# A three-layer graph network on one core: when VectorE reads a visit's sums, five buffers of one-hots, and GpSimd's scaling

## What is computed

```python
def _mean_agg(x, src, dst, n):
    msg_sum = jax.ops.segment_sum(x[src], dst, num_segments=n)
    cnt = jax.ops.segment_sum(jnp.ones((src.shape[0], 1), x.dtype), dst, num_segments=n)
    return msg_sum / jnp.maximum(cnt, 1.0)

def _sage_conv(x, src, dst, Wl, bl, Wr):
    agg = _mean_agg(x, src, dst, x.shape[0])
    return agg @ Wl.T + bl + x @ Wr.T
...
h = jnp.maximum(_layernorm(x, axis=-1), 0.0)
h = _sage_conv(h, src, dst, Wl0, bl0, Wr0)          # 128 -> 256
h = jax.nn.relu(_batch_norm(h, gamma0, beta0))
h = _sage_conv(h, src, dst, Wl1, bl1, Wr1)          # 256 -> 256
h = jax.nn.relu(_batch_norm(h, gamma1, beta1))
h = _sage_conv(h, src, dst, Wl2, bl2, Wr2)          # 256 -> 128
return x + jax.nn.log_softmax(h, axis=-1)
```

## Time and profile before

| | us |
|---|---|
| median of 3 runs (1485.67 to 1491.87) | 1490.81 |
| the profiled execution's own time | 1489.97 |
| its span, first to last instruction | 1488.2 |

### The profile page before, as it was taken

One profiled execution on the slowest core, in us unless ns is written; L12 is line 12 of the kernel. 1 busy time (PEld: TensorE's weight loads), 2 busy tenths in 40 slices (PEclk: granted clock), 3 DMA queues, 4 the chain that ended last, 5 costly groups with the idle time before them and its releaser, 6 DMA issues.

```text
span 1488.2 us, 36176 instructions
## 1 busy us (share of the span) xinstructions
PE 1330.0 (89%) x16035; PEld 855.4 (57%) x16035; DVE 603.8 (41%) x1131; ACT 519.4 (35%) x848; POOL 561.1 (38%) x562
## 2 busy tenths in 40 slices
PE   1387888898788889999999999999999899999997
PEld 1276777677677678665444444444446764444445
DVE  6977767677777984222011111111111211212223
ACT  4886766867687685441000000000000330000001
POOL 3313130321304000001766666665663015666650
PEclk9999989989999999999999999999999999999999
DMA  5234533543544354136667666665663479898983
GB/s 162 94 144 153 188 150 138 200 156 134 192 178 181 118 187 179 50 126 226 222 197 241 205 226 229 221 217 200 217 215 109 115 260 323 309 328 298 334 314 96
DMA packets 92007, 291.45 MB, mean 196 GB/s; under 512 B 17538, under 2 KB 53012, under 8 KB 88612
## 3 DMA queue, kind: packets, MB, share of 16 engines
q1 hardware_dynamic: 63596, 228.73, 42.9%
q0 software_dynamic: 21824, 55.44, 12.0%
q10 hardware_dynamic: 6424, 4.88, 1.1%
HBM read 197.78 MB, written 91.22 MB: 194 GB/s over the span
## 4 chain that ended last, share of the span: by engine, by line
PE 72%; issue 8%; ACT 7%; DMA 6%; DVE 4%; POOL 4%; ACTq 0%; SPq 0%; DVEq 0%; POOLq 0%
PE bank L1621 25%; PE bank L1198 14%; PE cells L1621 12%; PE cells L1188 5%; DMA hots<-table,src_i 3%; PE bank L1866 3%; ACT ring L652 3%; POOL hots L516 3%; PE cells L1233 2%; PE cells L1687 2%; PE bank L1624 2%; ACT junk L600 2%; DMA parts<-in_pairs_dram,last_i 1%; PE cells L1699 1%; PE bank L1206 1%
## 5 line engine op out<-in xcount | busy, mean ns | idle before, releaser
L516 POOL DMA_INDIRECT hots<-table,src_i x444 | 420.9, 948 | 458.1 <-DMA table<-parts 224.6
L1621 PE MATMUL bank<-ring,parts 128*128 128x500 f16 x2058 | 460.1, 373 | 0.0
L652 ACT CAST ring<-cells 128x980 f16<-128x980 f32 (+1 forms) x325 | 335.5, 1057 | 140.8 <-PE cells L1188 137.1
L1198 PE MATMUL bank<-ring,parts 64*128 64x250 f16 x4900 | 336.7, 279 | 14.3 <-issue 8.6
L1621 PEld LDWEIGHTS bank<-ring,parts 128*128 128x128 f16 x2058 | 191.9, 96 | 223.8 <-issue 9.4
L1198 PEld LDWEIGHTS bank<-ring,parts 64*128 64x128 f16 x4900 | 238.1, 98 | 39.2 <-issue 19.3
L877 DVE TENSOR_TENSOR hots<-iotas,tab 128x980 f16<-128x980 f16 (+3 forms) x262 | 247.4, 998 | 26.0 <-PE cells L1188 13.6
L1621 PE MATMUL cells<-ring,parts 128*128 128x500 f16 (+1 forms) x980 | 215.9, 373 | 0.0
L723 ACT ACTIVATE agmg<-cells,isp 128x124 f32<-128x124 f32 x20 | 7.3, 365 | 471.1 <-PE cells L1242 471.1
L1188 PE MATMUL cells<-hots 64*128 64x49 f16 x4670 | 110.0, 188 | 67.4 <-DVE hots L877 35.0
L1621 PEld LDWEIGHTS cells<-ring,parts 128*128 128x128 f16 (+1 forms) x980 | 90.9, 96 | 112.7 <-issue 9.0
(11 more groups left out here) (211 smaller groups left out, 1000.1 us busy)
## 6 DMA issues: line engine op xcount, KB each, us to landing
ring<-c_blocks SPq DMA_DIRECT2D x120, 750.0 KB, 6.1
c_blocks<-ring SPq DMA_DIRECT2D x25, 3062.5 KB, 10.7
ring<-c_blocks SPq DMA_DIRECT2D x40, 812.5 KB, 6.7
rcb<-rc_row SPq DMA_DIRECT2D x69, 125.0 KB
hots<-table,src_i POOLq DMA_INDIRECT x444
Z<-in_x_dram SPq DMA_DIRECT2D x4, 768.0 KB, 6.3
table<-parts SPq DMA_DIRECT2D x2, 1536.0 KB
table<-parts ACTq DMA_DIRECT2D x2, 1536.0 KB
```

The lines of the kernel that those rows point to most:

```text
L516: pool.indirect_dma_start(out=got[layer][:, 5 * (r % NGOT) + i, :], out_offset=None, in_=tables[layer], in_offset=bass.IndirectOffsetOnAxi ...
L652: act.copy(blk[c % 2][:, :, :].rearrange("p a (d g) -> p a d g", d=GD)[:, :, :, GPS * i:GPS * i + n], cells[t % 2][:, :, 0:n * NA].rearran ...
L1198: ins = pe.matmul(bank[2 + h][:, 0:BD], small[rows, a, part, :], blk[c % 2][rows, a, :], start=(a, part) == (0, 0), stop=(a, part) == (FUL ...
L1621: ins = pe.matmul(bank[b][:, 0:2 * BD].rearrange("p (s d) -> p s d", s=2), lhs, ring[0:r, :, BD * a:BD * a + BD], start=(a, part) == (0, 0 ...
```

## The change

- VectorE reads the sums of block c-2 in step 6 of visit c instead of step 2 (`dve_sums0`: copy and addition only). TensorE's wait in step 1 is as it was.
- The multiplication by the reciprocal counts goes to GpSimd (`mean0`, step 7 of visit c), with the semaphore `means` in place of `v_mean`; for the last block VectorE does it. The factor 1/1024 goes into the weights `wl[0]`, which VectorE scales beside `wr[0]`.
- NHOT is 5 instead of 4. Two of the buffers now lie in `early`, and two small arrays move (`grow` into `src_i`, `gspare` into `smp_i`).
- The table of a batch from the third on is made in steps 5, 6 and 7 of its visit, one instruction each, instead of all three in step 7.

Left out below are the hunks in which `v_mean` only becomes `means`, and the one that moves the two small arrays.

```diff
@@ -21,7 +21,7 @@
 EPS = 1e-5
 S0 = 1024.0
 GPH = 20
-NHOT = 4
+NHOT = 5
 NBT = 4
 NTAB = 8
 NG1 = 4
@@ -87,6 +87,8 @@
             chores.update({t0 + 18: ("rows", q + 1, 0), t0 + 31: ("windows", q + 1, 0), t0 + 33: ("ends", q + 1, 0), t0 + 41: ("tile", q + 1, 0),
                            t0 + 42: ("place", q + 1, 0), t0 + 46: ("table", q + 1, 0)})
 
+
+    table_at = {t + k: (k, chores[t][1]) for t in list(chores) if chores[t][0] == "table" for k in ((-2, -1, 0) if chores[t][1] > 1 else (0,))}
     turn_step = {c: t for t, (what, _, c) in chores.items() if what == "turn"}
 
     quarters = [(NA * k // 4, NA * (k + 1) // 4) for k in range(4)]
@@ -300,13 +302,14 @@
         xres = upper.rearrange("p (a f) -> p a f", a=NA)
         X = Z[:, 1, :].rearrange("p (a f) -> p a f", a=NA)
         HOT = GPH * (NA + P)
-        need = NBT * 256 + NBT * 3 * P + HOT // 2
-        early = upper if NA * 128 >= need + WE else sb("early", [P, need + WE])
+        need = NBT * 256 + NBT * 3 * P + HOT
+        early = upper if NA * 128 >= need else sb("early", [P, need])
         win = early[:, 0:NBT * 256].bitcast(I32).rearrange("p (w n two) -> p w n two", w=NBT, two=2)
         wrk = early[:, NBT * 256:NBT * (256 + 3 * P)].rearrange("p (k n e) -> p k n e", k=3, e=P)
-        hots = sb("hots", [P, NHOT - 1, HOT], F16)
-        hot = [early[:, NBT * (256 + 3 * P):need].bitcast(F16)] + [hots[:, k, :] for k in range(NHOT - 1)]
-        later = hots[:, :, :].rearrange("p k n -> p (k n)") if (NHOT - 1) * HOT >= 8960 else sb("later", [P, 8960], F16)[:, :]
+        hots = sb("hots", [P, NHOT - 2, HOT], F16)
+        hot = [early[:, need - HOT + HOT // 2 * k:need - HOT + HOT // 2 * (k + 1)].bitcast(F16) for k in range(2)] + \
+            [hots[:, k, :] for k in range(NHOT - 2)]
+        later = hots[:, :, :].rearrange("p k n -> p (k n)") if (NHOT - 2) * HOT >= 8960 else sb("later", [P, 8960], F16)[:, :]
         got = [None] + [later[:, 0:5 * NGOT * w].rearrange("p (s f) -> p s f", s=5 * NGOT) for w in rowf[1:]]
         agmg = sb("agmg", [P, 2, BD])
         gsum = sb("gsum", [P, 256])
@@ -532,7 +535,7 @@
             pool_ends(0)
             pool_rows(1)
             pool_windows(1)
-            for t in range(NST * NB):
+            for t in range(NST * (NB + 1)):
                 what, q, _ = chores.get(t, ("", 0, 0))
                 if what == "rows":
                     pool_rows(q)
@@ -542,6 +545,9 @@
                     pool_ends(q)
                 elif what == "place" and q > 1:
                     pool_place(q)
+                c, i = divmod(t, NST)
+                if c >= 2 and i == 7:
+                    mean0(pool, c - 2)
                 if t in ln_at and ln_at[t] in act_groups:
                     pool_lo(ln_at[t])
                 if t == TG - 20:
@@ -782,21 +788,27 @@
                 dve.tensor_scalar(wrk[:, 1, 0:n, HE * h:HE * h + HE], wrk[:, 0, 0:n, HE * h:HE * h + HE], float(h), -1024.0,
                                   ALU.is_equal, ALU.mult).then_inc(v_place, 1)
 
-        def dve_table(q, own):
+        def dve_table(q, k, own):
+
             n = batches[q][1] - batches[q][0]
             pen, hi = wrk[:, 1, 0:n, :], wrk[:, 2, 0:n, :].bitcast(I32)
+            c0, c1 = batches[q]
             if q > 1:
                 dve.wait_ge(p_place, 2 * (q - 1))
             else:
                 dve.wait_ge(v_place, 2 * (q + 1))
-            dve.wait_ge(v_tile, q + 1)
-            c0, c1 = batches[q]
-            dve.tensor_reduce(cntg[:, c0:c1, :], pen.rearrange("p n (d e) -> p n d e", d=GD), AX.X, ALU.add).then_inc(v_own, 1)
-            dve.wait_ge(v_own, own.up())
-            dve.scalar_tensor_tensor(pen, hi, 1024.0, pen, ALU.add, ALU.add).then_inc(v_own, 1)
-            own.up()
-            dve.scalar_tensor_tensor(wrk[:, 2, 0:n, :], hi, -128.0, win[:, 0:n, :, 0],
-                                     ALU.mult, ALU.add).then_inc(v_table, 1)
+            if k == -2 or q <= 1:
+                dve.tensor_reduce(cntg[:, c0:c1, :], pen.rearrange("p n (d e) -> p n d e", d=GD), AX.X, ALU.add).then_inc(v_own, 1)
+                own.up()
+            if k == -1 or q <= 1:
+                dve.wait_ge(v_tile, q + 1)
+                dve.wait_ge(v_own, own.n)
+                dve.scalar_tensor_tensor(pen, hi, 1024.0, pen, ALU.add, ALU.add).then_inc(v_own, 1)
+                own.up()
+            if k == 0:
+                dve.wait_ge(v_own, own.n)
+                dve.scalar_tensor_tensor(wrk[:, 2, 0:n, :], hi, -128.0, win[:, 0:n, :, 0],
+                                         ALU.mult, ALU.add).then_inc(v_table, 1)
 
         def loose_part(q):
 
@@ -878,7 +890,7 @@
                                         place.unsqueeze(2).to_broadcast((P, q, w, 2)), ALU.is_equal)
             ins.then_inc(v_hot, 1)
 
-        def dve_mean0(c, own):
+        def dve_sums0(c, own):
 
             mean = agm[:, c % 2, 0, :].rearrange("p (g d) -> p g d", d=GD)
             first, last = (bank[2 + h][:, 0:BD].rearrange("p (d g) -> p g d", d=GD) for h in range(2))
@@ -886,10 +898,12 @@
             dve.tensor_copy(mean, first).then_inc(v_own, 1)
             dve.wait_ge(v_own, own.up())
             dve.tensor_tensor(mean, last, mean, ALU.add).then_inc(v_halves, 1)
-            dve.wait_ge(v_halves, c + 1)
-            dve.wait_ge(d_rcb[c % 2], 16 * (c // 2 + 1))
-            dve.scalar_tensor_tensor(mean, mean, 1.0 / S0, rcb[:, c % 2, :].rearrange("p (g d) -> p g d", d=GD), ALU.mult,
-                                     ALU.mult).then_inc(v_mean, 1)
+
+        def mean0(eng, c):
+
+            eng.wait_ge(v_halves, c + 1)
+            eng.wait_ge(d_rcb[c % 2], 16 * (c // 2 + 1))
+            eng.tensor_tensor(agm[:, c % 2, 0, :], agm[:, c % 2, 0, :], rcb[:, c % 2, :], ALU.mult).then_inc(means, 1)
 
         def dve_mean(v, banks, scale, sums_no, col=0):
 
@@ -1063,7 +1077,7 @@
             dve_shift(0, 0)
             dve_tile(0)
             dve_place(0)
-            dve_table(0, own)
+            dve_table(0, 0, own)
             for c in range(NB + 1):
                 for i in range(NST):
                     t = NST * c + i
@@ -1079,7 +1093,8 @@
                         dve_count(0, own)
                     elif t == 6:
                         dve.wait_ge(d_w, 16 * 7)
-                        dve.tensor_scalar(wr[0][:, :, :], wr[0][:, :, :], 1.0 / S0, None, ALU.mult).then_inc(v_wr0, 1)
+                        for w0 in (wr[0], wl[0]):
+                            dve.tensor_scalar(w0[:, :, :], w0[:, :, :], 1.0 / S0, None, ALU.mult).then_inc(v_wr0, 1)
                     if t in ln_at and ln_at[t] in vec_groups:
                         dve_norm(ln_at[t])
                     what, q, b = chores.get(t, ("", 0, 0))
@@ -1095,12 +1110,12 @@
                         dve_tile(q)
                     elif what == "place" and q <= 1:
                         dve_place(q)
-                    elif what == "table":
-                        dve_table(q, own)
                     elif what == "count":
                         dve_count(q, own)
-                    if c >= 2 and i == 2:
-                        dve_mean0(c - 2, own)
+                    if t in table_at:
+                        dve_table(table_at[t][1], table_at[t][0], own)
+                    if c >= 2 and i == 6:
+                        dve_sums0(c - 2, own)
                     b = made0.get((c, i - 6))
                     if b is not None:
                         dve_stats(0, b)
@@ -1145,7 +1160,9 @@
                     elif (c, i) == (NB, 6):
                         dve.wait_ge(t_isp, 2)
                         dve.tensor_copy(isp[:, :], bank[4][:, P:P + 1]).then_inc(v_isp, 1)
-            dve_mean0(NB - 1, own)
+            dve_sums0(NB - 1, own)
+            dve.wait_ge(means, NB - 1)
+            mean0(dve, NB - 1)
             dve.wait_ge(t_tot, 1)
             dve.tensor_scalar(cut[:, 0:1], bank[6][:, 0:1], float(E), None, ALU.is_equal).then_inc(v_own, 1)
             dve.wait_ge(v_own, own.up())
@@ -1302,9 +1319,9 @@
                         done = upto
                     b = made0.get((c, i))
                     if b is not None:
-                        pe.wait_ge(v_mean, b + 1)
+                        pe.wait_ge(means, b + 1)
                         pe.wait_ge(a_h0, min(c - 1, NG))
-                        pe.wait_ge(v_wr0, 1)
+                        pe.wait_ge(v_wr0, 2)
                         if b:
                             pe.wait_ge(a_z, 2 * b)
                         pe_linear0(b)
```

More of the change, by code:

```diff
@@ L318, in gnn_program @@
         base_i = sb("base_i", [P, 2], I32)
-        grow = early[:, need:need + 256].bitcast(I32)
+        grow = src_i[:, 0:256].bitcast(I32)
         gwin = early[:, 0:2 * WE].rearrange("p (n two) -> p n two", two=2)
-        gspare = early[:, need:need + WE]
-        assert 2 * WE <= NBT * (256 + 3 * P)
+        gspare = smp_i[:, 0:WE // 2].bitcast(F16)
```

(19 more changed lines are left out.)

## The result

The changed kernel takes 1565.09 us (median of 4 runs, 1563.01 to 1569.2), the kernel before 1488.24 us on the same chip: ratio 1.0522, 95% interval 1.0481 to 1.0563, so slower by 5.2%. The forecast was 1565 us.

What follows compares the result with a forecast made beforehand. No engine is full in layer 0; what ends TensorE's waits decides. 95 - 31.4 - 5 - 5 + 20 + 1.8 = 75 us over 1489.97 gave 1565 us, range 1527 to 1612.

Steps and rivals of the forecast that it cites:

- pauses at the read: TensorE's step-1 wait for VectorE's later read of the sums in layer 0: some 16 large pauses, +95 us.
- idles for issue: TensorE running out of instructions while the 3 MB store moves: 2.1 us absorbed in each of 15 visits, -31.4 us.
- one-hots: TensorE's waits for VectorE's one-hots, 14.0 us: about 5 behind the weight scaling go, -5 us.
- clock: TensorE's clock drops after pauses: 2.7 us each for 16 pauses, less 23 lost already, +20 us (ends 0 and 52).
- Rows and windows: Step-5 chores waiting for ScalarE, ahead of the read: 32.0 us in five rows visits, 25.5 in five windows visits.
- The read behind two lots and two steps of the table: Visits 4, 8, 12, 16, 20, where VectorE is already late: 5.0 us lost in visit 8, 28.3 in all.
- The first visit of a batch: Visits 5, 9, 13, 17, 21: the first lot waits for a turned table, so the read ends late; loss 9.3 us.
- Other visits: loss 0: Remaining layer 0 visits: VectorE is ahead, the fifth buffer letting it make step 6's lot before TensorE ends the visit.
- GpSimd's scaling: Multiplication moved to GpSimd, at most 1.78 us; TensorE asks for the mean some 9 us later, so 0 on the path.
- the pauses are not absorbed: Rival, chance 0.16: idles for issue return later in the visit, or each pause drops the clock; 1596, up to 1634 us.
- the pauses cost less: Rival, chance 0.10: later visits run without waits, half of the 95 us returns, clock term 0; 1493 to 1535 us.
- VectorE's lead wins: Rival, chance 0.03: with five buffers the reads come in time, and waits of 14.0 and 5.6 us go; 1470 us.

## Why the prediction was right, point by point

**The mechanism** was right, the nearness of the number in part luck. The read stands behind chores that cannot end before TensorE is already waiting, and the experiments with the read at steps 2, 4 and 6 show it from both sides. The terms of the sum, in us; those measured are differences of the two profiles' waits, the clock that of TensorE's busy time in layer 0:

| term | forecast | measured |
|---|---|---|
| pauses at the read | +95 | +106.5 (112.1 - 5.6) |
| idles for issue | -31.4 | -30.1 (46.1 to 16.0) |
| ScalarE's copies | -5 | -6.7 (8.7 to 2.0) |
| one-hots | -5 | +0.5 (`hots` and `parts`: 16.4 to 16.9; the forecast's 14.0 was `hots` alone) |
| clock | +20 | +7.9 |
| wl0's scaling | +1.8 | +0.1 (visit 1's store at 86.10, now 86.17) |
| sum | +75 | +78, layer 0 grew by 73.5 |

So the total is better than its parts: the pauses (11.5 us too low), the one-hots (5.5 too low) and the clock (12.1 too high) were off and made up for each other. The idles for issue leave out the one of 3.0 us before 294.88 in the earlier trace rows, which is gone in the changed kernel; with it they go from 49.1 to 16.0 us, and the sum is 75.

*Rows and windows.* Forecast 32.0 and 25.5; the pauses are 7.47, 6.37, 6.37, 6.27, 6.28 (32.8 in all) and five times 5.00 (25.0). The working from the earlier trace rows holds.

*The read behind two lots and two steps of the table.* Forecast 28.3 over the 5.6 of before, so 33.9; measured 7.19, 8.25, 6.54, 8.05, 9.89, together 39.9. More than half of the 6 us over the forecast fell in visit 8 (8.25 instead of 5.0). There only the table's 1.31 us was counted, and not what its first instruction waits for. In visit 8, VectorE:

```profile
239.82 2.06 DVE L889 TENSOR_TENSOR hots<-iotas,tab 128x2560 f16<-128x2560 f16 x2
244.00 0.69 DVE L801 TENSOR_REDUCE cntg<-parts 128x8 f32<-128x512 f32 x1 [2.12 <-POOL parts L501]
244.60 2.06 DVE L889 TENSOR_TENSOR hots<-iotas,tab 128x2560 f16<-128x2560 f16 x2
246.58 0.69 DVE L806 SCALAR_TENSOR_TENSOR parts<-parts 128x512 f32<-128x512 int32 x1
247.18 0.41 DVE L898 COPY agm<-bank 128x250 f32<-128x250 f32 x1
247.63 0.42 DVE L900 TENSOR_TENSOR agm<-bank,agm 128x250 f32<-128x250 f32 x1
```

GpSimd, the pair of "place" instructions:

```profile
237.67 6.29 POOL L501 TENSOR_SCALAR parts<-parts 128x256 f32<-128x256 f32 x2 [2.80 <-DVE parts L774]
```

The first table instruction waits 2.12 us for GpSimd, whose two instructions take 6.29 us together, where two of the mean length in the earlier trace rows take 3.6. They run while VectorE makes lots. In step 7, where it stood, this wait had room; ahead of the read it is on the path. With the table in one step visit 8 pauses 4.78 us: 3.5 less, the 1.31 and the 2.12 together. In the other four visits the pair takes 3.5 us, as it mostly did before, and the table does not wait. What the rest of the 6 us comes from was not separated; with the statistics at step 10 the five pauses fall to 31.0, so VectorE's rest behind the read, below, has a part in them.

*The first visit of a batch.* Forecast 9.3; measured 0.84, 0.83, 0.84, 1.64 and 4.72, together 8.9.

*Other visits: loss 0.* Visits 22 to 24 lose 5.6 us. The fifth buffer was given as the reason for 0; with four buffers it is the same, so that reason falls. What was overlooked is VectorE's rest behind the read, first of its three waits for ScalarE:

```profile
DVE st L999 <- ACT Z L702: 96.9, 24, 5.5
DVE row L746 <- ACT junk L606: 35.0, 5, 8.4
DVE off L753 <- ACT junk L614: 25.6, 5, 6.9
```

Its statistics wait 96.9 us in 24 visits. Before, the read stood two lots ahead of them; now they stand right behind it, VectorE rests until TensorE, just released, has come to step 2 and ScalarE has moved its result out, and the next read stands seven lots further. With the statistics at step 10 those three pauses go.

*The clock.* Forecast +20, and by TensorE's busy time 7.9. The pauses do drop the clock. Visit 6, the pause and the ten us behind it (columns as in the earlier trace rows):

```profile
187.77:194.13 6.36, 0.00 (x0) 0.03 (x1) 3.10 (x6) 3.02 (x6) 2.35 (x2) 0.80 1.04 431
194.13:204.13 10.00, 10.00 (x257) 9.52 (x258) 5.84 (x9) 7.10 (x8) 3.28 (x4) 0.79 0.37 69
```

The mean over the ten us behind each of the 16 large pauses is 0.78, or 2.2 us of clock each and 35 in all, where 2.7 and 43 were taken from the earlier trace rows. What failed is in the main the size of this price: the mean of three idles, two of 3 us and one of 2.5, put on pauses twice as long. In a long pause part of the lower clock falls on the pause itself, where it costs nothing: in 15 of the 16 the clock is already down before TensorE goes on, 23 us of lost clock in all. So the lost clock in layer 0 grows by far more (0.06 of 518 us, now 0.11 of 591.5: 31 and 65 us) than TensorE's busy time does. By the Trainium skill's rule (TensorE: Matmul & The Clock Gate, HAM oscillation) each pause throttles: here the 16 long ones agree, with 0.72 to 0.87 behind them; the dear end of the term, +52, was far off.

*What the pauses give back.* The term "issue" was right in size, and its cause is shown: paced in four parts, the same store takes these idles from 46.1 to 5.2 us. That it is instructions that come late can be read in the trace of the kernel before, which has a DMA queue for them (packets, MB and share in layer 0 from 86 us on):

```profile
q8 instruction: 86, 1.41, 1.1%
```

Its packets are of 16 KB, one in 6 us on the mean. Taken packet by packet, all 23 idles for issue (the one before 294.88 included) end 1.2 to 1.6 us after one of them has landed, and so do the 11 that are left in the changed kernel (1.1 to 1.5).

*One-hots.* Five us at the weight scaling went as forecast, but in visits 4, 8, 12, 16, 20 TensorE now waits 0.64 to 1.33 us for a lot (4.1 in all), where it waited 0.35 us in visit 16 alone.

*GpSimd's scaling* cost nothing on the path, as forecast: 0.88 us on the mean in 24 instructions, no wait of TensorE's on it, and no effect that can be told, together with the rest of the change, with the read back at step 2.

*Rivals.* That the pauses are not absorbed is refuted by the idles themselves, 46.1 to 16.0 us, and by the four-part store, which gains 2.85% in the kernel before and at most a little in the changed one. That the pauses cost less, half of them coming back, falls with the table of terms: 36.8 of the 106.5 us come back. That VectorE's lead wins, and that it does nothing, fall with the result.

## What to carry to other kernels

Before a step is moved on an engine that works in order, list all that it is moved past and ask of each what it waits for; if one of these needs the engine that waits for the moved step, a lead of buffers cannot help. Where sums have a single buffer, their read is what the writer waits for next, so nothing should stand ahead of it that is not already done. And an idle that the profile calls issue deserves a look at the transfers under way, those of the instructions too: here one store in four parts was worth 2.85%, more than any order of VectorE's work that was tried.

## What the runs showed of the hardware

The instructions of TensorE came late while a 3 MB store moved: 46.1 us of idles in layer 0, each ending just after a 16 KB packet of instructions had landed, and 5.2 us when the store was issued in four parts three steps apart, with the same bytes. The Trainium skill (Runtime: NRT & Kernel Launch, Instruction fetch mechanics) has the crossing from block to block mostly hidden; these runs differ from it as long as such a store is under way, and agree without it.

GpSimd's first 256-element operation of a "place" pair took 2.25 us in four visits of the changed kernel and 5.15 in visit 8, in the old kernel with the late read 7.12 twice. In visit 8 the VectorE lots beside it stayed at 2.06; where it took 2.25, the lot beside it took 2.25 to 2.27 instead. The Trainium skill (SBUF — State Buffer, Who interferes with whom) says that a VectorE instruction with two inputs in SBUF contends with a GpSimd instruction that reads SBUF, and that the one that comes second waits until the first ends. The trace agrees in kind: both inputs of the lots are in SBUF, and now GpSimd pays, now VectorE.
